# The order of the first DMA requests in a four-layer graph network kernel

## The reference, cut to what matters

```python
# layer 0, h = max(layernorm(x), 0)
q, k = split(h @ Wqk)
v = h @ Wv
agg = adj @ (k * mask)
w = (1 / sqrt(512)) * mask * rowsum(q * agg)
x = x + softmax(w, over the nodes)[:, :, None] * v
# layer 1, h = max(layernorm(x), 0)
query = h @ Wq.T + bq;  keyt = h @ Wk.T + bk;  value = h @ Wv.T + bv
weight = adj * exp(query @ keyt.T);  weight = weight / rowsum(weight)
x = x + weight @ value
```

## Time and profile before

| | |
|---|---|
| median of 3 runs | 2223.53 us (2223.47 to 2223.89) |
| the profiled execution's own time | 2223.11 us |
| its span | 2221.3 us |
| PE busy | 2203.8 us (99%) |
| DVE, ACT, POOL busy | 1356.5, 776.6, 740.4 us |
| mean DMA traffic | 99 GB/s over the span |

### The profile page before, as it was taken

The page is one execution under the profiler, slowest core; times in us unless marked ns, Lnnn a source line. Parts: engine busy times, 40 slices in busy tenths (PEclk is TensorE's granted clock), DMA queues, the critical chain, the costliest instruction groups (busy, mean ns, idle before and its releaser), DMA issues.

```text
span 2221.3 us, 39182 instructions
## 1 busy us (share of the span) xinstructions
PE 2203.8 (99%) x15756; PEld 1759.2 (79%) x15756; DVE 1356.5 (61%) x2712; ACT 776.6 (35%) x1393; POOL 740.4 (33%) x926
## 2 busy tenths in 40 slices
PE   8999999999999999999999999999999999999999
PEld 5788888888888888888888888888877777777776
DVE  4575666666665676555655454555687575757542
ACT  3433333233323333333322333232444343434342
POOL 1443433343433423332322332332343131313130
PEclk9999999999999999999999999999999999999999
DMA  6333332333333344433233323333443323233321
GB/s 211 77 80 101 96 103 84 86 95 89 87 92 94 102 136 126 114 86 94 83 101 100 106 82 95 88 97 92 144 151 112 105 87 103 88 100 92 95 60 38
DMA packets 142006, 220.52 MB, mean 99 GB/s; under 512 B 33920, under 2 KB 40064, under 8 KB 141824
## 3 DMA queue, kind: packets, MB, share of 16 engines
q1 hardware_dynamic: 135680, 209.62, 32.5%
q10 hardware_dynamic: 6144, 8.40, 1.6%
HBM read 84.71 MB, written 50.37 MB: 61 GB/s over the span
## 4 chain that ended last, share of the span: by engine, by line
PE 97%; DVE 2%; DMA 1%; issue 0%; SPq 0%; POOL 0%; ACT 0%; DVEq 0%; ACTq 0%; POOLq 0%
PE bank L326 54%; PE bank L316 32%; PE bank L342 3%; PE bank L559 3%; PE bank L496 1%; PE bank L466 1%; PE bank L363 1%; PE bank L306 1%; DVE yt L946 1%; PE bank L545 0%; DMA wq<-in_L_gnn_Wq_w 0%; DMA x<-in_x 0%; DVE hs L636 0%; DVE stA L611 0%; SPq L968 0%
## 5 line engine op out<-in xcount | busy, mean ns | idle before, releaser
L326 PE MATMUL bank<-w_hi,h3T_hi 128*128 128x512 f32 x768 | 305.6, 398 | 0.0
L326 PE MATMUL bank<-w_lo,h3T_hi 128*128 128x512 f32 x768 | 299.4, 390 | 0.0
L326 PE MATMUL bank<-w_hi,h3T_lo 128*128 128x512 f32 x768 | 299.1, 389 | 0.0
L975 ACT ACTIVATE Z<-bank 64x512 f32<-64x512 f32 x256 | 151.8, 593 | 320.5 <-PE bank L326 246.9
L326 PEld LDWEIGHTS bank<-w_hi,h3T_hi 128*128 128x128 f32 x768 | 144.1, 188 | 55.1 <-issue 26.0
L989 ACT ACTIVATE hn<-x,stA 128x512 f32<-128x512 f32 x192 | 141.6, 825 | 106.9 <-POOL stA L1234 106.9
L326 PEld LDWEIGHTS bank<-w_hi,h3T_lo 128*128 128x128 f32 x768 | 144.2, 188 | 30.4
L326 PEld LDWEIGHTS bank<-w_lo,h3T_hi 128*128 128x128 f32 x768 | 144.2, 188 | 28.9
L636 DVE STREAM_TRANSPOSE hs<-hn 128x512 f32<-128x512 f32 x192 | 124.2, 690 | 38.7 <-ACT hn L989 38.7
L931 DVE TENSOR_TENSOR yt<-bank,bsumt 128x512 f32<-128x512 f32 x64 | 43.9, 685 | 164.2 <-PE bank L559 164.2
L1044 ACT ACTIVATE QQ<-bank,bqk 128x512 f32<-128x512 f32 x64 | 43.9, 689 | 283.5 <-PE bank L316 276.5
(11 more groups left out here) (201 smaller groups left out, 5853.3 us busy)
## 6 DMA issues: line engine op xcount, KB each, us to landing
hGA<-hs SPq DMA_DIRECT2D x760, 64.0 KB, 2.0
mid<-x SPq DMA_DIRECT2D x32, 1024.0 KB, 4.3
x<-mid SPq DMA_DIRECT2D x32, 1024.0 KB, 5.7
x<-in_x SPq DMA_DIRECT2D x16, 1024.0 KB, 5.8
hGB<-hs SPq DMA_DIRECT2D x256, 64.0 KB, 2.0
out<-x SPq DMA_DIRECT2D x15, 1024.0 KB, 4.6
PT<-hs SPq DMA_DIRECT2D x120, 64.0 KB, 2.0
PT<-hs ACTq DMA_DIRECT2D x120, 64.0 KB, 2.1
```

Of the source, the lines that this page charges most:

```text
L326: ins = eng.matmul(b[:], h[l][:, k, ts], W[r][:, k, :], start=(k == 0 and i == 0), stop=(last and k == 3 and i == 2))
L975: return eng.activation(dst, src, ACT.Copy)
```

## The change

SP's requests at the start get another order. The request for x of group 0 goes behind the first pieces of `qT` and `kTw` (the first quarter of the layer's query and key weights), and the request for `wq1` goes from behind the eight block requests of `gather(0, 0, (0, 1))` to ahead of them, right after `wk1`. Nothing else changes; the other engines' programs are the same.

```diff
             qk_rows = rows(L0_gnn_Wqk)
-            load_x(0, x_v[0])
             for k in range(4):
                 eng.dma_start(qT[:, k, :], qk_rows[:, k, :]).then_inc(d_qk[k], 16)
                 eng.dma_start(kTw[:, k, :], qk_rows[:, 4 + k, :]).then_inc(d_qk[k], 16)
+                if k == 0:
+                    load_x(0, x_v[0])
             eng.dma_start(bcol[:, 0:4], L1_gnn_Wq_b).then_inc(d_b1, 16)
             eng.dma_start(bcol[:, 4:8], L1_gnn_Wk_b).then_inc(d_b1, 16)
             eng.dma_start(mcol[:], nodemask_cols).then_inc(d_b1, 16)
             eng.dma_start(wk1[:], rows(L1_gnn_Wk_w)).then_inc(d_k1, 16)
+            eng.dma_start(wq1[:], rows(L1_gnn_Wq_w)).then_inc(d_q1, 16)
             gather(0, 0, (0, 1))
-            eng.dma_start(wq1[:], rows(L1_gnn_Wq_w)).then_inc(d_q1, 16)
             load_adj(0)
             load_mask(0)
```

## The result

The changed kernel is slower: 2226.81 us (median of 18 runs, 2225.53 to 2228.99) against 2223.16 (18 runs, 2222.71 to 2225.17), 3.65 us. The ratio is 1.0017, with a 95% interval of 1.0010 to 1.0023. The forecast was 1.9 us faster, and the range ended at 2223.2; that the move would stay within 0.2% held, its sign did not. The runs of the changed kernel are spread over 3.5 us, and the profiled execution (2228.99, span 2227.2) is the slowest of them; it shows the mechanism larger than the median has it (by 2.2 us in all).

The account below looks back on a forecast made before the run. PE was taken to bound the kernel (97% of the chain). Its 4.6 us gain was capped at the scores by x1 to 1.24 + 0.7 = 1.9 us, so 2223.53 would become 2221.6 us, range 2220.0 to 2223.2.

Parts of the forecast that it names:

- The first wait and wq1: PE's start: pair lands at 4.9, PE starts 2.9 us earlier; L387's 1.70 us wait for wq1 goes.
- both parts: At L387's end: the earlier pair and earlier wq1 together bring PE 2.9 + 1.7 = 4.6 us.
- The rise of PE's pace: PE's clock rise some 3.7 us after its first matmul moves with the start; otherwise 2.9 us bring only 1.45.
- all of the first 3.1 MB were still under way: At wk1's request, 7.11: x and all pieces still in the queue, so wq1 lands by 18, before PE asks.
- x lands when the pair did, 1.47 us later: First x behind the pair: same bytes in the other order, so x lands at 7.8, 1.47 us later than before.
- Pieces 1 to 3 land as before: Later weight pieces have the same bytes ahead, so they land as before, and PE reaches piece 1 after it lands.
- s = 0.7 us (0.4 to 1.3): How much earlier x1, the second x, lands once wq1's megabyte no longer stands ahead of it in the queue.
- rival C: x1 bound by its own later request, gain 0.4 at the scores, clock fall costs 1.8: 2224.9 us; chance 0.07.
- 7.4 us, 2.6 MB at 350 GB/s: Queue from Wv0's landing to x1's: Wv1, bias rows, x1, adjacency and mask, putting x1 at 37.1.
- The cover of 1.24 us and the new wait at L342: Before the scores: ACT's g0T copies end 1.24 us before PE asks; PE would then stand still 2.7 us.
- the gain is the smaller of PE's own and 1.24 + s: At the scores: gain is the smaller of 4.6 and 1.24 plus x1's earlier landing, giving 1.9 us.
- The clock: In the wait before the scores: granted clock falls, PE works the next 3.7 us at half speed, losing 1.8 us.

Follow-up runs that it names:

- e10: Changed kernel with the first x in four requests and ACT's g0T copies ahead of x1's normalisation: 2218.19 us, ratio 0.9977 to the kernel before.
- e1: Kernel before with only the pair moved ahead of x, wq1 left behind the blocks: 2228.42 us, ratio 1.0024.
- e3: Changed kernel with seven throwaway float32 products keeping PE busy in the wait before the scores: 2224.94 us, 1.9 faster than the changed kernel.
- e4: Changed kernel with ACT's g0T copies 2 and 3 ahead of x1's normalisation: 2219.33 us, ratio 0.9982 to the kernel before.
- e6: Changed kernel with the first x asked for as four requests of 256 KB: 2225.75 us, ratio 1.0009 to the kernel before.
- e2: Kernel before with only wq1 moved ahead of the blocks, x still first: 2222.26 us, ratio 0.9995.
- e5: Kernel before with ACT's g0T copies 2 and 3 ahead of x1's normalisation: 2223.45 us against 2223.61, ratio 0.9998.
- e7: Changed kernel with the first x asked for on ACT's queue and ACT's g0T copies first: 2221.31 us, ratio 0.9991 to the kernel before.
- e9: Kernel before with wq1 ahead of the blocks and ACT's g0T copies first, x still first: 2221.38 us, ratio 0.9991.
- e12: Changed kernel with the first x and x1 each in four requests, ACT's order unchanged: 2224.80 us, ratio 1.0006 to the kernel before.
- e8: Changed kernel with x1 asked for right behind Wv0, ahead of Wv1: 2220.56 us, ratio 0.9985 to the kernel before.
- e11: Changed kernel with first x in four requests, ACT's g0T copies first and x1 ahead of Wv1: 2218.72 us, ratio 0.9978 to the kernel before.

## Why the prediction was wrong, step by step

**The first wait and wq1: right.** The pair landed at 4.2 instead of 4.9, so PE gained 3.6 us at its start, not 2.9; L387's wait of 1.7 us went. In e10, where nothing takes them back, the scores start 5.2 us earlier, against my 4.6 for both parts. The rise of PE's pace moved with the start, as I had taken it: in e10 the weight loads are 0.85 us apart from 5.2 until 7.8, and 0.43 apart from 10.3 on (with gaps of either length between), while PE began at 4.2. It is read from this spacing alone; the granted clock of the windows stands at 1.00 there, in the earlier trace rows's stretch too. (That all of the first 3.1 MB were still under way when wk1 was asked for, at 7.11, was a misreading: x had landed at 6.35. Nothing came of it.)

**"x lands when the pair did, 1.47 us later": wrong, the first step that failed.** It landed at 10.24, in e1 at 9.00, in e3 at 9.25, in e4 at 10.44. I counted bytes and took it that the queue delivers them in the order of the requests. With x in four requests that gave the right time (7.86 in e6, 7.70 in e10). With the one request, 1.1 MB of what was asked for behind x had gone through before x was complete, where 0.3 had in the kernel before. "Pieces 1 to 3 land as before" fell, too: PE stopped 1.5 us for piece 1 in the changed kernel, and not in e6 or e10.

**s = 0.7 us (0.4 to 1.3): wrong, the step that set the sign.** s was -4.1 in the profiled execution of the changed kernel (-2.3 and -3.3 in e3 and e4, with the same requests). About 2.5 of that are the later x, by e6. But e6, with x at 7.86, has s = -1.6, and e2, with nothing late and wq1 out of the way, 0.9 with a request 1.1 us earlier. What rival C had as its condition, x1 bound by its own later request, held within a microsecond in every kernel in which the order just ahead of it was left alone: from request to statistics 11.1 us before, 11.7 changed, 12.0 or less in e1, 11.3 in e2, 11.5 in e3, 10.8 in e4, 10.9 in e5, 12.1 in e6, 10.4 in e7, 10.8 in e9, 11.5 in e10, 11.3 in e12. These runs can't tell x1's own request from the one for Wv0, which moves with it (14.4 us from Wv0's request to the statistics before, 14.9 changed, 14.3 in e2, 15.1 in e6). Only another place among the requests (e8, Wv1's megabyte no longer ahead) made it shorter, 9.3 us or less.

The term that was mis-sized stands out in e6, where all ahead of it came true: Wv0 asked for at 24.18 (24.06 in my sum) and there at 30.01 (29.7). From there to x1 I had 7.4 us, 2.6 MB at 350 GB/s; it took 9.2:

```profile
30.01:39.25 9.24, 9.24 (x42) 7.66 (x41) 1.29 (x2) 4.25 (x8) 5.05 (x4) 1.00 1.02 323
```

These are 3.0 MB at 323 GB/s: the pace was lower than in the kernel before, and more was moved ahead of x1's end than I had counted. The x of group 2, asked for at 31.75, was in the queue as well; which bytes they were is not shown.

**The cover of 1.24 us and the new wait at L342: right in place, wrong in size.** The wait stands where I put it, with 6.2 us instead of 2.7. The rule "the gain is the smaller of PE's own and 1.24 + s" holds with what was measured: 1.24 - 4.08 = -2.84 against a start of the scores 2.89 us late, and 1.24 - 1.57 = -0.33 against 0.38 late in e6. PE came to the wait 3.3 us earlier than before and left it 2.9 us later: the 6.2.

**The clock: a rival's term that came true.** My sum has no such term, since I took the wait to swallow everything ahead of it and did not ask what it does to the work behind it. C priced a fall in the wait at 1.8 us; the longer scores and products cost 2.6 in the profiled execution, and 1.9 in e6, whose wait is 5.7 us. C as a whole came to 2224.9, with 0.07; the true case is C with a wait longer by what the late x adds. The chance was too low, since I took the place of x in the queue as known to a tenth of a microsecond and put no bound on it, although no row showed a 1 MB request behind a short one at the start, and the rows of those behind other megabytes should have warned me: Wv0, asked for at 23.24, took 7.8 us, and x1 11.1.

**The price of a megabyte.** The megabyte of Wv0 into a short queue took 5.6 (changed kernel) and 5.8 us (e2), the first x behind the pair 8.6 (changed kernel). The Trainium skill ("DMA: Bandwidth & Descriptors", Anatomy of one DMA) gives 2.0 us and bytes at 436 GB/s for the GpSimd path, an estimate of 4.4 us for a megabyte; these requests, which SP makes, took longer, and the measurement decides.

## What to carry to other kernels

Before moving a load, follow both what waits for it and what stands behind those waits in the in-order programs: here two copies that PE needs stood behind a normalisation that they do not need, and a cover of 1.2 us hid it. Where a kernel gains or loses through one late input, put the consumers that don't need it ahead of it first; the moved loads then pay (3.8 us here, where they cost 3.7, and 5.0 with the first x in four requests besides). A transfer's landing behind another can't be taken from bytes alone: requests behind it can go through ahead of its end, so bound it by its own request's time, too.

## What the runs showed of the hardware that I had not expected

A 1 MB load of 512 runs of 2 KB behind a 0.5 MB pair took 7.4 to 8.8 us from request to landing in five kernels (changed, e1, e3, e4, e8), and as four loads of 256 KB 5.9 to 6.2 us from the first request (e6, e10, e11, e12). Bytes of later requests passed it, 1.1 MB of them in the changed kernel; why is not shown.

Two transfers on two queues, asked for at the same time, were done at nearly the same time (7.2 and 7.6 us, e7, one profile): the smaller one got no lead.

PE's idle time cost more than itself: after waits of 6.2, 5.7 and 4.5 us the scores took 3.68 us instead of 2.02 (the changed kernel, e6, e12), after one of 6.9 us L387 and L306 took 2.7 us more (e1), and idle PE filled with products whose result is thrown away was 1.9 us faster than idle PE (e3). A wait of 1.3 us cost nothing more (e8: granted clock 1.00 and the scores in 2.08 us, as in the same view of the kernel before).
